# Folding the pair logits through VectorE and memory instead of TensorE, and doing their softmax input half a step later

## The reference, cut to what matters

```python
x = x + 0.5 * ffn(layernorm(x))
x = x + attention(layernorm(x))
x = x + 0.5 * ffn(layernorm(x))

# ffn: a cluster and a token count only where a softmax over 64 clusters passes a threshold
dots = softmax(x @ centroids.T / 0.1)
hits = dots > 0.01
query_sel, cluster_sel = any(hits, axis=1), any(hits, axis=0)
out = where(query_sel[:, None] & cluster_sel[assignments][None, :], x @ weight.T + bias, 0)
```

## Time and profile before

| what | before |
|---|---|
| median of 3 runs | 1193.3 us (1192.45 to 1193.41) |
| the profiled execution | 1196.15 us, span 1194.3 us |
| PE busy | 1181.7 us, 99% of the span |
| DVE busy | 799.3 us, 67% |
| ACT busy | 499.2 us, 42% |
| POOL busy | 441.0 us, 37% |

### The profile page before, as it was taken

One profiled execution on the slowest core, in us unless ns is written; L12 is line 12 of the kernel. 1 busy time (PEld: TensorE's weight loads), 2 busy tenths in 40 slices (PEclk: granted clock), 3 DMA queues, 4 the chain that ended last, 5 costly groups with the idle time before them and its releaser, 6 DMA issues.

```text
span 1194.3 us, 24986 instructions
## 1 busy us (share of the span) xinstructions
PE 1181.7 (99%) x10072; PEld 1002.5 (84%) x10072; DVE 799.3 (67%) x1272; ACT 499.2 (42%) x718; POOL 441.0 (37%) x582
## 2 busy tenths in 40 slices
PE   7999999999999999999999999999999999999998
PEld 6888888888888888888888888888888878888887
DVE  6654554455444477787777877778777774199987
ACT  5232233222211355656656656565565663211110
POOL 1335445543424643433434334344343210051332
PEclk9999999999999999999999999999999999999999
DMA  8578777876565366565565666565655565017885
GB/s 275 144 206 232 207 206 193 225 211 182 164 189 159 98 169 169 148 171 146 160 166 139 181 152 152 160 155 164 161 142 164 129 169 193 2 72 259 279 304 195
DMA packets 344978, 208.73 MB, mean 175 GB/s; under 512 B 289440, under 2 KB 308640, under 8 KB 344864
## 3 DMA queue, kind: packets, MB, share of 16 engines
q1 hardware_dynamic: 329696, 187.73, 56.2%
q10 hardware_dynamic: 15168, 19.40, 4.7%
HBM read 118.49 MB, written 88.60 MB: 173 GB/s over the span
## 4 chain that ended last, share of the span: by engine, by line
PE 91%; DMA 3%; DVE 2%; issue 1%; ACT 1%; SPq 1%; POOL 1%; POOLq 0%; DVEq 0%
PE ps_b L285 9%; PE ps_q L285 8%; PE ps_q L287 8%; PE ps_q L286 8%; PE ps_b L287 8%; PE ps_b L286 8%; PE ps_a L285 8%; PE ps_a L287 8%; PE ps_a L286 8%; PE ps_t L292 6%; PE ps_q L1450 3%; PE ps_q L299 2%; PE ps_q L301 2%; PE ps_q L1425 2%; DMA y_scratch<-xa 1%
## 5 line engine op out<-in xcount | busy, mean ns | idle before, releaser
L318 POOL TENSOR_TENSOR var_eps<-moments,eps 128x1 f32<-128x1 f32 x96 | 18.2, 190 | 396.6 <-DVE moments L314 396.6
L285 PE MATMUL ps_a<-w_hi,odd_hi 128*128 128x512 f32 x368 | 147.7, 401 | 0.0
L287 PE MATMUL ps_a<-w_hi,odd_lo 128*128 128x512 f32 x368 | 143.8, 391 | 0.0
L286 PE MATMUL ps_a<-w_lo,odd_hi 128*128 128x512 f32 x368 | 143.2, 389 | 0.0
L635 POOL TENSOR_SCALAR f_out<-f_out,token_on 128x1024 f32<-128x1024 f32 x30 | 85.6, 2852 | 75.6 <-DVE f_out L1013 75.3
L686 POOL TENSOR_TENSOR x_ring<-x_ring,f_tmp 128x1024 f32<-128x1024 f32 x32 | 77.3, 2414 | 91.2 <-DVE best L1159 58.5
L285 PE MATMUL ps_b<-proj_hi,y_hi 128*128 128x512 f32 x256 | 103.3, 403 | 0.0
L287 PE MATMUL ps_b<-proj_hi,y_lo 128*128 128x512 f32 x256 | 100.0, 391 | 0.0
L286 PE MATMUL ps_b<-proj_lo,y_hi 128*128 128x512 f32 x256 | 99.7, 390 | 0.0
L327 ACT ACTIVATE y_tok<-x_ring,norms 128x1024 f32<-128x1024 f32 x64 | 79.7, 1245 | 38.0 <-ACT o_head L881 21.0
L737 POOL TENSOR_TENSOR late<-late,mask 128x1024 f32<-128x1024 f32 x18 | 44.1, 2463 | 137.3 <-DMA late<-x_scratch 91.6
(11 more groups left out here) (219 smaller groups left out, 3113.1 us busy)
## 6 DMA issues: line engine op xcount, KB each, us to landing
xa<-in_L_attn_x SPq DMA_DIRECT2D x32, 512.0 KB, 5.0
f_tmp<-f_scratch SPq DMA_DIRECT2D x32, 512.0 KB, 4.2
x_ring<-in_L_attn_x SPq DMA_DIRECT2D x32, 512.0 KB, 3.6
f_scratch<-f_out SPq DMA_DIRECT2D x30, 512.0 KB, 4.0
x_scratch<-x_ring SPq DMA_DIRECT2D x30, 512.0 KB, 3.5
y_scratch<-xa SPq DMA_DIRECT2D x28, 512.0 KB, 4.6
ya_tok<-y_scratch SPq DMA_DIRECT2D x112, 128.0 KB, 3.3
late<-x_scratch SPq DMA_DIRECT2D x22, 512.0 KB, 6.7
```

The costliest lines, as they stand in the source:

```text
L285: pe.matmul(acc, hi[:, k, :], w_h[:, k, cols], start=(k == 0), stop=False)
L286: pe.matmul(acc, hi[:, k, :], w_l[:, k, cols], start=False, stop=False)
L287: last = pe.matmul(acc, lo[:, k, :], w_h[:, k, cols], start=False, stop=(k == KB - 1))
```

## The change

For the 15 pairs whose logits are worked out in the odd steps 5 to 33, the two turning matmuls on PE are gone. Instead ACT's copy puts the columns in another order, DVE turns blocks of 32 by 32 in place (`pair_turn`, in the even step), SP stores the tile to a scratch in memory and loads it back with the blocks rearranged (`store_pair`, and four DMAs in `load_pair`), and DVE's `pair_soft_in` adds the two halves directly from `pair_sums` in SBUF. `pair_soft_in` moves from the start of the even step to the middle of the following odd step, the exponential to the even step after, and `pair_soft_out` two steps on. PE's waits for the softmax become waits for ACT's copy of the pair before. The very last pair is still folded on PE.

The core of the diff:

```diff
         def pair_soft_in(dve, u):
...
+            if by_memory(u):
+                parts = pair_sums[:, :].rearrange("p (s h t c) -> p s t h c", s=2, h=2, c=D)
+                dve.wait_ge(pair_in, 64 * (u - NP + 1) + 16)
+                wait(dve, soft_exp, u)
+                dve.tensor_tensor(pair_exp_in[:, :].rearrange("p (t h c) -> p t h c", h=2, c=D), parts[:, 0], parts[:, 1],
+                                  ALU.add).then_inc(soft_step, 2)
...
+        def pair_turn(dve, u):
+            dve.wait_ge(pair_copied, u + 1)
+            dve.transpose(pair_sums[:, :], pair_sums[:, :]).then_inc(pair_turned, 1)
...
+                def store_pair(u):
+                    sp.wait_ge(pair_turned, u - NP + 2)
+                    sp.dma_start(pair_d, pair_sums[:, :]).then_inc(pair_stored, 16)
+
+                def load_pair(u):
+                    sp.wait_ge(pair_stored, 16 * (u - NP + 2))
+                    for b in range(T4):
+                        sp.dma_start(pair_sums[D * b:D * b + D, :].rearrange("p (h x) -> p h x", h=T4),
+                                     pair_d.rearrange("(h q) (b x) -> b q h x", q=D, b=T4)[b]).then_inc(pair_in, 16)
...
+                    if i >= 6 and i % 2 == 0:
+                        store_pair(NP + (i - 6) // 2)
+                    if i > NT and i % 2 == 0:
+                        load_pair(NP + (i - 6) // 2)
...
+                        if i >= 6 and i % 2 == 0:
+                            load_pair(NP + (i - 6) // 2)
...
                     if i >= 6 and i % 2 == 0:
-                        pair_soft_in(dve, NP + (i - 6) // 2)
+                        pair_turn(dve, NP + (i - 6) // 2)
...
-                    if i >= 7 and i % 2 == 1:
-                        pair_soft_out(dve, 1, NP + (i - 7) // 2)
+                    if i >= 9 and i % 2 == 1:
+                        pair_soft_out(dve, 1, NP + (i - 9) // 2)
...
+                    if i >= 7 and i % 2 == 1:
+                        pair_soft_in(dve, NP + (i - 7) // 2)
                     if 0 <= i - 2 < NT:
                         dve.transpose(probs[:, :], probs[:, :]).then_inc(probs_ready, 1)
...
+                pair_soft_out(dve, 1, 2 * NP - 3)
+                pair_soft_in(dve, 2 * NP - 2)
                 low_third(LAST)
...
-                        pe.wait_ge(soft_in, u)
+                        pe.wait_ge(soft_in, NP)
+                        pe.wait_ge(pair_copied, u)
                         pair_logits(pe, odd_hi, odd_lo).then_inc(pair_done, 1)
...
-                    if 0 <= i - 4 < NT - 2 and i % 2 == 1:
-                        fold_pair(NP + (i - 4) // 2)
```

More of the change, by code:

```diff
@@ L47, in macaron_kernel @@
     o_d = nc.dram_tensor("o_scratch", (NT, HKV, P, D), F32, kind="Internal").ap()
+    pair_d = nc.dram_tensor("pair_scratch", (P, 2 * P), F32, kind="Internal").ap()
     STREAMED = list(range(0, NT - 2, 2))
@@ L190, in logit_at, with by_memory @@
         def logit_at(u):
-            return ps_q[:, 0, 0:QUARTER] if NP <= u < 2 * NP - 1 else ps_q[:, 3, QUARTER:HALF]
+            return ps_q[:, 3, QUARTER:HALF]
+        def by_memory(u):
+            return NP <= u < 2 * NP - 1
         def half(h):
@@ L240, in macaron_kernel @@
         late_in = w_in[0:6]
+        pair_stored, pair_in, pair_turned = w_in[6], w_in[7], cen_hi
         y_last_stored = cen_in
@@ L332, in pair_soft_in @@
         def pair_soft_in(dve, u):
-            parts = logit_at(u).rearrange("p (t s c) -> p s t c", s=2, c=NCL)
             logits = pair_exp_in[:, :].rearrange(BY_TILE, c=NCL)
[L336 to L340, removed]
+            if by_memory(u):
[4 more added lines that the diff above has]
+                                  ALU.add).then_inc(soft_step, 2)
+            else:
+                parts = logit_at(u).rearrange("p (t s c) -> p s t c", s=2, c=NCL)
+                dve.wait_ge(folded, u + 1 - (NP - 1 if u > NP else 0))
+                wait(dve, soft_exp, u)
+                dve.tensor_copy(logits, parts[:, 0]).then_inc(soft_step, 1)
+                dve.wait_ge(soft_step, 7 * u + 1)
+                dve.tensor_tensor(logits, logits, parts[:, 1], ALU.add).then_inc(soft_step, 1)
             dve.wait_ge(soft_step, 7 * u + 2)
@@ L764, in copy_pair @@
                     act.wait_ge(pair_done, u + 1)
-                    act.copy(pair_sums[:, :], pair_ps).then_inc(pair_copied, 1)
+                    if by_memory(u):
+                        act.wait_ge(soft_in, u)
+                        act.copy(pair_sums[:, :].rearrange("p (b t c) -> p t b c", t=2, c=D),
+                                 pair_ps.rearrange("p (t b c) -> p t b c", t=2, c=D)).then_inc(pair_copied, 1)
+                    else:
+                        wait(act, soft_in, u if u > NP else 0)
+                        act.copy(pair_sums[:, :], pair_ps).then_inc(pair_copied, 1)
                 def move_kv(k):
@@ L913, in _ @@
                         last.then_inc(k_ready, 1)
-                    if i >= 6 and i % 2 == 0:
-                        pair_soft_exp(act, NP + (i - 6) // 2)
+                    if i >= 8 and i % 2 == 0:
+                        pair_soft_exp(act, NP + (i - 8) // 2)
                     if i == NT + 2:
@@ L945, in _ @@
                 keep_third(3)
+                pair_soft_exp(act, 2 * NP - 2)
                 high_third(LAST)
@@ L1442, in _ @@
                             pe.wait_ge(m_mask, 1)
-                        pe.wait_ge(soft_in, NP + max(0, (i - 4) // 2))
+                        pe.wait_ge(soft_in, NP)
                         scores_of = ps_scores.rearrange("p r (t j e) -> p r t j e", j=2, e=D)
@@ L1499, in _ @@
                 pe.wait_ge(scores_read, NT)
-                pe.wait_ge(soft_in, 2 * NP - 1)
+                pe.wait_ge(pair_copied, 2 * NP - 1)
                 pair_logits(pe, odd_hi, odd_lo).then_inc(pair_done, 1)
```

## The result

The change costs time. The median goes from 1193.18 us (four runs, 1192.45 to 1193.41) to 1217.65 us (four runs, 1210.71 to 1224.86), a ratio of 1.0197 with an interval of 1.0174 to 1.0219. The forecast was 1222.0, its range 1198 to 1228. The direction and the time came out as said, but two parts of the sum are wrong, with opposite signs: it has too many blocked steps, and it leaves out the clock.

The account below looks back on a forecast made before the run. PE was taken as the bound, busy 99% of the span, with DVE nearly so in odd steps. 11 x 2.75 + 2 x 0.71 - 15 x 0.22 = +28.4 us, making the median 1221.7, said as 1222; range 1198 to 1228.

Parts of the forecast that it names:

- blocked steps: Odd steps where POOL's two-input addition holds up DVE's softmax input; 11 of 13 were forecast, PE waiting 2.75 us in each.
- The fold: Two turning matmuls on PE removed for each of fifteen pairs: 0.22 us each, 3.3 us off PE.
- The slack and the undisturbed step: Odd steps: DVE has 0.14 us to spare before PE waits; three added instructions take 0.85, so PE waits 0.71 us.
- The block: Odd step: a DVE instruction with two SBUF inputs stands until POOL's earlier two-input addition ends; PE waits 2.75 us.
- SP's queue: Four loads ahead of other transfers take 1.3 to 2.3 us against slack 2.2; POOL's addition stays or comes 0.1 later.
- half the blocks: Rival: the input tile comes later, so POOL's addition misses DVE's three instructions in about half the steps; +18.2, 1211.5 us, chance 0.12.
- The end of the stage: Store landing and loads ahead of the last load of the heads: between 0 and 2.7 us, taken as 0.

Follow-up runs that it names:

- fourth experiment: Changed kernel with the softmax input behind the value projection's reading and SP's four loads between the query-and-key store and its wait; 1192.14 us, ratio 0.9974 to before.
- second experiment: Changed kernel with only SP's four pair loads moved, between the query-and-key store and the wait for it; 1243.2 us, ratio 1.0398 to the kernel before.
- sixth experiment: Changed kernel with SP's loads issued in its idle time and DVE's three instructions altered so none has two SBUF inputs; 1204.49 us, ratio 1.0062 to before.
- third experiment: Changed kernel with SP's loads issued in its idle time and POOL's two-input addition replaced by a one-input multiplication; 1209.04 us, ratio 1.0114 to before.
- fifth experiment: Kernel before, fold left on PE and nothing through memory, only the softmax input moved to the middle of the odd step; 1228.78 us against 1196.36, ratio 1.0254.
- first experiment: Changed kernel with only the softmax input moved, behind the reading of the value projection; 1194.22 us against 1194.74 for the kernel before, ratio 0.999.

## Why the prediction was right, and where not

**The fold.** Right: 0.22 a fold, seen at the end of the odd step and, by itself, in the 3.1 us of the fourth experiment.

**The slack and the undisturbed step.** Right: a step without a block leaves PE a gap of 0.64 to 0.77 where 0.71 was said. The two of 1.25 to 1.30 have another cause: there the load of the values, which stands behind the four loads on SP, was late and DVE waited for it, 1.46 and 1.40 us.

**The block.** Right in kind and size: 2.46 to 2.89 a step here, 2.75 on the mean in the second experiment, where 2.75 was said. It was said of the addition; here POOL was late enough that in three of four blocked steps it was the subtraction that stood. The Trainium skill, "SBUF — State Buffer", section "Who interferes with whom", says that VectorE's second SBUF input uses a port that it shares with GpSimd and that whoever has it keeps it; the addition of 2.46 us beside POOL's two-input one, and the sixth experiment without such an instruction, agree. The third experiment doesn't agree with it as far as a one-input instruction goes: VectorE was through 1.25 us after the start of one that lasts 2.86. The prediction took the earlier trace rows to mean that POOL's one-input instruction doesn't hold DVE. It does hold it, at its beginning; L344 had come 1.81 us after its start.

**SP's queue.** This is the step that failed. It was said that `add_first` "stays where it is, or comes 0.1 later", from a slack of 2.2 us at a landing of 3.5 and issues of 1.3 to 2.3. The issues were as said, 2.03. But the landing of 3.5 was the median of all 30 stores, and that median hides two kinds. By the landing times in the trace of before, the 12 stores on which the odd steps' additions hang took 3.5 to 5.2 us, and those in between mostly about 3.0; the very store of the earlier trace rows took 3.9. So the slack was 0.7 to 2.3, not 2.2. It was then used up twice: the store itself went out 1.7 later, and it landed so late that the load went out 5.1 to 6.3 us after it in 9 of the 12 steps, at the moment of the landing. So 8 of the 12 came after the three instructions, and one of the nine, at 5.14, only just before. The rival "half the blocks" named this mechanism and had 0.12. With 4 blocked steps the gaps are 18.0 us and not 31.7. Why the store lands in 3.8 to 6.3 us is not settled; in the second experiment, with the four loads out of the way, it is 3.5 to 5.0, but the transfers that share the time were not taken apart.

**The clock.** A term that the sum didn't have. Each of the 4 long gaps is followed by a stretch at the lower level, 6.3 us together. The earlier trace rows shows the upper level everywhere, but of a kernel in which PE has no gap of this length in that stage; the price of a wait was taken as its length, and here it is its length and some 1.5 us. In the second experiment the two terms together, 31.6 - 3.3 + 9 x 1.5, give 42 us, and the span is 43.8 longer.

**The end of the stage.** Taken at 0, and it is no loss: its last intervals are 1.3 shorter.

**Together.** 28.4 was said. Gaps came out 13.7 lower, the clock 6.3 higher, folds and last steps 0.9 better: 28.4 - 13.7 + 6.3 - 0.9 = 20.1, against 19.7 in the profiled run. That the time is near the forecast is luck in part: the clock, which the sum leaves out, makes good for almost half of the missing blocks, and the medians are 4.8 us further apart than the two profiled runs. Without the clock that run would lie 13.4 us over before, under the 18.2 of the rival "half the blocks". The runs of the changed kernel spread over 14 us and those of before over 1. A varying number of blocked steps would do that. The mean granted clock points that way, 0.997 in the fastest of the four, 0.994 in two and 0.990 in the slowest: a fall of 3.4 us to half lowers it by 0.0014, so an estimate from these figures is 2, 4, 4 and 7 falls. But there is a trace of one run only, so this is argued and not shown.

## What to carry to other kernels

An instruction put on a side engine is priced by what runs beside it at that place, so lay the other engine's timeline under it: three instructions of 0.9 us in all cost 2.7 a step beside POOL's addition, 0.8 without an instruction of two SBUF inputs, and nothing after the one that PE waits for. Ask of every DMA issue what is queued behind it, and use the landing time of that very transfer, late ones included, not the median of its kind. When an idea loses, take it apart before dropping it: the way through memory was good, and with its softmax input behind the value projection's reading and its loads in SP's own wait it beats the kernel before by 0.26%.

## What the runs showed of the hardware

- Beside a one-input POOL instruction of 128x1024 (2.86 us, third experiment) a DVE instruction with two SBUF inputs was through 1.25 to 1.36 us after POOL's start; beside a two-input one (2.41 us) it ended 0.14 to 0.16 us after POOL's recorded end in all 27 such steps of three runs.
- One PSUM operand is enough to pass: a subtraction of 0.29 us with its second input in PSUM took 0.29 beside POOL's addition (sixth experiment), with both in SBUF 1.3 to 2.3 (fifth).
- Clock falls in the attention stage followed PE's gaps of 2.02 us and more: 4 times for 4 blocked steps of the changed kernel, 9 times for 11 in the second experiment and 6 times for 12 in the fifth. After gaps of up to 1.84 there was none. A fall lasted about 3.4 us and cost about 1.5. The length of the gap alone doesn't decide: 2.02 was followed by a fall in the fifth experiment, 2.69 and 2.71 in the second were not. In the first stage, too, a wait of 1.93 us in the first experiment was followed by the lower level, and one of 2.21 at the same place in the fourth was not.
